# Sixteen layers on one core: batches normalised in the next layer's front, ternary layers as one stream, a cell with two gate bank sets

## The reference

```
x = x + f_i(layernorm(x))        # i = 0..15
layernorm(x) = (x - mean) / sqrt(var + 1e-5), over the 128 features
```

```
# layers 5, 7 (W1, W2 rounded to -1, 0, 1 beforehand)
h = relu(x @ W1.T + b1)          # 128 -> 512
out = h @ W2.T + b2              # 512 -> 128
# layers 13, 15: 32*64 tokens, here 4 batches of 512; the state c goes from batch to batch
f = sigmoid(x@wf.T + c@uf.T + bf); i = sigmoid(x@wi.T + c@ui.T + bi)
g = tanh(x@wc.T + c@uc.T + bc);    c = f*c + i*g
h = tanh(x@wo.T + c_final@uo.T + bo)   # once the last c is there, for all tokens
```

## Time and profile before

| | us |
|---|---|
| timed, 3 runs | 3011.98, 3024.86, 3028.07; median 3024.86 |
| profiled execution, its own time | 3016.8 |
| its span, first to last instruction | 3015.0 |
| TensorE busy | 2417.6 (80%) |
| VectorE busy | 1804.8 (60%) |
| ScalarE busy | 1277.7 (42%) |
| GpSimd busy | 644.2 (21%) |
| mean granted TensorE clock | 0.879 of full speed |

### The profile page before, as it was taken

How to read it: one execution, slowest core, us unless ns; L and a number is a source line. 1 busy time by engine, 2 the same in 40 slices (tenths; PEclk the granted TensorE clock), 3 DMA queues, 4 the chain that set the end, 5 groups by cost and what they waited for, 6 DMA issues and landing times. The chain is left out here.

```text
span 3015.0 us, 30344 instructions
## 1 busy us (share of the span) xinstructions
PE 2417.6 (80%) x9626; PEld 1001.7 (33%) x9626; DVE 1804.8 (60%) x2866; ACT 1277.7 (42%) x2512; POOL 644.2 (21%) x736
## 2 busy tenths in 40 slices
PE   8999999476699897776767399877779979777777
PEld 3333334122122343532333144322324437322223
DVE  5666654478777345424434644488884437378894
ACT  3555641276477312113222043265554312255562
POOL 1111110222111101100001010065551012055560
PEclk9999999688799998885669589888899979889889
DMA  3000000221000200000000000000000000000000
GB/s 137 1 1 1 1 1 1 32 38 17 1 1 1 84 1 1 1 0 0 0 0 1 0 0 0 1 0 1 1 0 1 0 1 2 1 0 0 0 1 14
DMA packets 9356, 25.90 MB, mean 9 GB/s; under 512 B 1072, under 2 KB 7280, under 8 KB 8176
## 3 DMA queue, kind: packets, MB, share of 16 engines
q1 hardware_dynamic: 8336, 23.18, 2.7%
q10 hardware_dynamic: 864, 0.79, 0.2%
HBM read 16.56 MB, written 1.05 MB: 6 GB/s over the span
## 5 line engine op out<-in xcount | busy, mean ns | idle before, releaser
L2599 PE MATMUL l_py<-l_read,w_const 128*128 128x512 f32 x512 | 316.3, 704 | 93.1 <-DVE l_read L2732 74.2
L2876 POOL TENSOR_TENSOR l_drive<-l_du,l_bsb 128x512 f32<-128x512 f32 x256 | 325.9, 1296 | 207.0 <-ACT l_bsb L2673 187.7
L2723 DVE TENSOR_TENSOR_SCAN l_state<-l_decay,l_drive 128x512 f32<-128x512 f32 x256 | 310.5, 1213 | 58.9 <-ACT l_decay L2681 51.4
L398 ACT ACTIVATE l_probs<-l_psp,l_stats 128x512 f32<-128x512 f32 x256 | 172.9, 682 | 150.6 <-DVE l_stats L408 150.6
L2681 ACT ACTIVATE l_decay<-l_delta,l_a 128x512 f32<-128x512 f32 x256 | 176.3, 689 | 136.1 <-DVE l_state L2723 135.7
L2599 PEld LDWEIGHTS l_py<-l_read,w_const 128*128 128x128 f32 x512 | 99.8, 215 | 246.9 <-DVE l_read L2732 204.1
L249 POOL TENSOR_TENSOR l_nx_small<-l_nx_small,w_const 128x4 f32<-128x4 f32 x27 | 27.2, 1009 | 717.2 <-DVE l_nx_small L243 717.2
L1267 DVE TENSOR_REDUCE l_tops<-l_ring 128x2 f32<-128x1024 f32 x128 | 151.5, 1220 | 46.0 <-PE l_ring L1258 45.6
L406 DVE TENSOR_REDUCE l_stats<-l_psp 128x2 f32<-128x1024 f32 x128 | 156.2, 1221 | 35.8 <-PE l_psp L360 35.1
L714 DVE SCALAR_TENSOR_TENSOR l_product<-l_psu,w_gated,l_first 128x512 f32<-128x512 f32 x104 | 78.1, 751 | 158.4 <-ACT l_first L688 158.1
L2732 DVE TENSOR_TENSOR l_read<-l_state,l_pc 128x512 f32<-128x512 f32 x256 | 168.4, 658 | 0.0
(11 more groups left out here) (510 smaller groups left out, 4624.7 us busy)
## 6 DMA issues: line engine op xcount, KB each, us to landing
l_stack<-l_parts SPq DMA_DIRECT2D x84, 64.0 KB
w_gated<-in_gated SPq DMA_DIRECT2D x1, 3297.5 KB, 10.5
w_mha<-in_mha SPq DMA_DIRECT2D x1, 2568.5 KB, 13.3
w_ssm<-in_ssm SPq DMA_DIRECT2D x2, 1171.0 KB, 15.6
w_moe<-in_moe SPq DMA_DIRECT2D x1, 2248.0 KB, 18.2
w_const<-in_const SPq DMA_DIRECT2D x1, 1325.0 KB, 7.6
x<-x_in SPq DMA_DIRECT2D x1, 1024.0 KB, 4.9
out<-x SPq DMA_DIRECT2D x1, 1024.0 KB, 3.9
```

Source lines behind the costliest of these rows:

```text
L398: act.activation(probs[:, s % 4, i, :], psp[:, s % 2, i, :], ACT.Exp, bias=stats[:, s % 4, 1, i:i + 1], scale=scale, accum_out=stats[:, s ...
L2599: pe.matmul(py[:, t, :], eye, read[:, s % 4, :], start=n == 0, stop=n == NS - 1, skip_group_check=True)\
L2723: dve.tensor_tensor_scan(state[:, s % 4, :], decay[:, s % 2, :], drive[:, s % 4, :], 0.0, ALU.mult, ALU.add).then_inc(L["state"].sem, 1)
L2876: pool.tensor_tensor(drive[:, s % 4, :], du[:, b % 2, t, :], bsb[:, n % 2, :], ALU.mult)\
```

## The change

- `NextNorm` can have more than one bank and then keeps a buffer per bank, so a batch's centre needn't wait for the norm of the one before.
- `NORMALISES_NEXT` gains 5 and 7, so the standalone norms n6 and n8 go; n0, n3, n7, n9, n11, n14 and n15 stay. `NORMALISES_LAST` gains 4, 5, 12 and 13: layers 3, 4, 11 and 12 normalise three batches, and layers 4, 5, 12 and 13 the fourth in their front (`late`, one centre to scale for batch 3).
- `routed_ffn`: scoring of the batches goes between the first up projections, and var, eps, spread and scale come one step later.
- `bit_ffn` is one stream of 16 steps over all batches with three buffers, two out banks and the norms inside, and reads xn without a copy.
- `cell` has two sets of gate banks, two answer banks and two h buffers; f*c is computed as soon as f is there.

The core of the diff ("..." for what is left out):

```diff
-    def __init__(self, L, bank, steps=1, last=False):
+    def __init__(self, L, *banks, steps=1, last=False):
...
+    def bank(self, b):
+        return self.banks[(b - self.first) % len(self.banks)]
+    def free(self, b):
+        return max(b - self.first - len(self.banks) + 1, 0)
...
# routed_ffn, TensorE
                 if last_in:
                     late.centre(pe, B - 1)
-                for b in range(B - 1):
-                    score(pe, b)
                 up(pe, 0)
+                up(pe, 1)
                 if last_in:
                     late.var(pe, B - 1)
-                up(pe, 1)
+                score(pe, 0)
                 up(pe, 2)
+                score(pe, 1)
                 if last_in:
                     late.spread(pe, B - 1)
                 up(pe, 3)
-                score(pe, B - 1)
+                score(pe, 2)
+                score(pe, 3)
...
-                    if normed(n, 3) is not None:
-                        nx.var(pe, normed(n, 3))
-                    if normed(n, 6) is not None:
-                        nx.spread(pe, normed(n, 6))
+                    if normed(n, 4) is not None:
+                        nx.var(pe, normed(n, 4))
+                    if normed(n, 7) is not None:
+                        nx.spread(pe, normed(n, 7))
... # VectorE: eps 4 -> 5, scale 8 -> 9; keep stays at 3, diag at 6
# linear_attention (4): centre first; var after project(0, 0); spread after turn_keys(0, 1);
#   VectorE keep ahead of the angles, eps after rotate(0, 0), diag after add_v(0), scale after take_states(0);
#   rstd on GpSimd after the MEMSETs. elu_attention (12) alike:
                     if is_batch(a):
                         project_q(pe, a)
                         project_k(pe, a)
+                        if a == 0 and last_in:
+                            late.var(pe, B - 1)
...
                     if is_batch(a):
                         turn_keys(pe, a)
+                        if a == 0 and last_in:
+                            late.spread(pe, B - 1)
...
                 pool.memset(state[:, :, :, :, :], 0.0).then_inc(L["blank"].sem, 1)
+                if last_in:
+                    late.rstd(pool, B - 1)
                 for a in range(B + 2):
...
# bit_ffn, new
+        def widen(pe, n):
+            b, m = divmod(n, FT)
+            if b == B - 1 and m == 0 and last_in:
+                pe.wait_ge(L["in_xn"].sem, L["in_xn"].at(0, 1))
+            pe.wait_ge(L["hidden"].sem, L["hidden"].at(0, max(n - 2, 0)))
+            pe.matmul(up[:, n % 3, :], w1[:, m * P:(m + 1) * P], core.xn[:, b * S:(b + 1) * S], start=True, stop=True)\
+                .then_inc(L["up"].sem, 1)
...
+                for n in range(END):              # END = N + 9
+                    if n < N:
+                        widen(pe, n)
+                    if 0 <= n - 2 < N:
+                        narrow(pe, n - 2)
+                    if n == 2 and last_in:
+                        late.var(pe, B - 1)
+                    if n == 5 and last_in:
+                        late.spread(pe, B - 1)
+                    if normed(n, 3) is not None:  # and centre 3, square 4, keep 4, var 5,
...                                               # eps and diag 6, spread 7, scale 8
# cell, new, TensorE
+                from_input(pe, 0)
+                from_state(pe, 0)
+                if last_in:
+                    late.var(pe, B - 1)
+                from_input(pe, 1)
+                if last_in:
+                    late.spread(pe, B - 1)
+                for b in range(1, B):
+                    from_state(pe, b)
+                    if b + 1 < B:
+                        from_input(pe, b + 1)
+                    else:
+                        answer_input(pe, 0)
+                        answer_input(pe, 1)
... # VectorE: late.diag and late.scale behind the first c
-NORMALISES_NEXT = (0, 1, 3, 4, 9, 11, 12)
-NORMALISES_LAST = (1, 3, 9, 11)
+NORMALISES_NEXT = (0, 1, 3, 4, 5, 7, 9, 11, 12)
+NORMALISES_LAST = (1, 3, 4, 5, 9, 11, 12, 13)
```

More of the change, by code:

```diff
@@ L1901, in _ @@
                         rotate(dve, a, 0)
+                        if a == 0 and last_in:
+                            late.eps(dve, B - 1)
                     if is_batch(o):
@@ L1906, in _ @@
                         add_v(dve, a)
+                        if a == 0 and last_in:
+                            late.diag(dve, B - 1)
                     if is_batch(o):
@@ L1984, in _ @@
             def _(pe):
[L1985 to L1993 removed]
+                if last_in:
+                    late.centre(pe, B - 1)
@@ L2002, in _ @@
                             .then_inc(L["hidden"].sem, 1)
+                    if normed(n, 4) is not None:
+                        nx.square(act, normed(n, 4))
             @block.vector
             def _(dve):
-                for b in range(B):
-                    take_normed(dve, L, b, xn[:, :])
-                    dve.wait_ge(L["down"].sem, L["down"].at(b, FT))
-                    dve.scalar_tensor_tensor(out=core.batch(b), in0=out[:, :], scalar=b2, in1=core.batch(b),
-                                             op0=ALU.add, op1=ALU.add).then_inc(L["done"].sem, 1)
+                if last_in:
+                    late.keep(dve, B - 1)
+                    late.eps(dve, B - 1)
+                    late.diag(dve, B - 1)
+                    late.scale(dve, B - 1)
@@ new lines, in _ @@
+                for n in range(END):
+                    if normed(n, 2) is not None or n == N + 2 and inner < B:
+                        b = (n - 2) // FT - 1
+                        x = core.x[:, b * S:(b + 1) * S]
+                        dve.wait_ge(L["down"].sem, L["down"].at(0, FT * (b + 1)))
+                        dve.scalar_tensor_tensor(out=x, in0=out[:, b % 2, :], scalar=b2, in1=x, op0=ALU.add,
+                                                 op1=ALU.add).then_inc(L["done"].sem, 1)
+                    if normed(n, 8) is not None:
+                        nx.scale(dve, normed(n, 8))
+                    if normed(n, 4) is not None:
+                        nx.keep(dve, normed(n, 4))
+                    if normed(n, 6) is not None:
+                        nx.eps(dve, normed(n, 6))
+                        nx.diag(dve, normed(n, 6))
@@ L2012, in bit_ffn, with _ @@
+            @block.gpsimd
+            def _(pool):
+                if last_in:
+                    late.rstd(pool, B - 1)
+                for b in range(inner):
+                    nx.rstd(pool, b)
     L.close()
@@ L2430, in _ @@
-                pe.wait_ge(L["state"].sem, L["state"].at(B - 1, 1))
-                for b in range(B):
-                    pe.wait_ge(L["answered"].sem, L["answered"].at(b, 0))
-                    pe.matmul(out[:, :], core.w(g, "wo"), core.normed(b), start=True, stop=False)
-                    pe.matmul(out[:, :], core.w(g, "uo"), c[:, :], start=False, stop=True)\
-                        .then_inc(L["answer"].sem, 1)
+                if last_in:
+                    late.centre(pe, B - 1)
@@ new lines, in _ @@
+                    dve.wait_ge(L["opened"].sem, L["opened"].at(0, 3 * b + 3))
+                    dve.tensor_tensor(ig[:, :], i_[:, :], n_[:, :], ALU.mult).then_inc(L["new"].sem, 1)
+                    dve.wait_ge(L["kept"].sem, L["kept"].at(0, b + 1))
+                    dve.wait_ge(L["new"].sem, L["new"].at(0, b + 1))
+                    dve.tensor_tensor(c[:, :], ig[:, :], h[:, 0, :], ALU.add).then_inc(L["state"].sem, 1)
+                    if b == 0 and last_in:
+                        late.diag(dve, B - 1)
+                        late.scale(dve, B - 1)
```

286 lines of the change are left out of this document (180 added, 106 removed).

## The result

The kernel after takes 2926.47 us (median of 4 runs, 2923.66 to 2933.32), the kernel before, run beside it, 3022.74; the ratio is 0.9689 with a 95% interval of 0.9657 to 0.9721. The forecast was 2929 us. In a later comparison the same code stood at 2918.53 against 3017.71, ratio 0.9675 (0.965 to 0.9699).

A forecast was written before the change was run, and what follows sets the result against it. Limits differ by place: TensorE in routed loops, engine-to-engine chains at tails and in the cell. Terms summed to -88.7 us from 3016.8, giving 2929 us; own range 2915 to 2943, wider range 2910 to 2960.

The forecast's parts named there:

- rival 1: Routed loops: the stall moves along with the later slots, so the loop saving is 0: 2958 us; chance 0.13.
- rival 3: Fronts wait as long as the old tails, so the norm stays on the path: about 2965 us; chance 0.05.
- rival 4: Slower: routed layers' steps run long at 1.2 GHz from cut scoring and denser TensorE work; 3049 us at 40%; chance 0.02.
- Rival 2: Routed and cell fronts keep a low clock: +3 instead of -8, layers 12, 13 2 us more each: 2944; chance 0.12.
- 1 and 2, tails and fronts: Tails of layers 3, 4, 11, 12 go: -39.3 us; moved norm costs +0.6 in layer 4, +2.2 in layer 12.
- the named cover: Layer 4's front: VectorE's late copy falls while the angles stand still for GpSimd's MEMSETs, so it costs 0.3 us.
- 3, ternary layers: Layers 5 and 7 as one stream, norm included: layer 5 51.0 us, 1.1 slower; layer 7 46.7 us, 1.8 faster.
- 4, routed loops: Layers 1, 3, 9, 11: later norm slots remove 24 TensorE stalls before variance and spread: -28.9 us, bounds 0 and 31.
- 5, routed fronts: Scoring between wide matmuls recovers half-clock loss in four fronts: -8 us of 10.2, layer 9 keeping 1.8; bounds -3 and 12.
- 6, the cell: Layers 13 and 15: rounds of 5.16, 5.16, 4.96 us instead of 6.19, answers 4.7 less: layer 15 -8.5, layer 13 -6.1.
- part 2: What the moved norm costs in the next layer's front: layer 4 +0.6 us, layer 12 +2.2 us.
- part 5: Routed layers' fronts by number, -8 us; the reference for layer 13's late norm cost, 2.4 us, means the cell.

The follow-up runs named there:

- e3: Kernel after, but layers 3, 4, 11 and 12 normalise their own last batch at their end again: 2951.29 us, ratio 0.9786.
- e5: Kernel after, with layers 6 and 8 also norming batches 0-2 inside, layers 7 and 9 taking the last, ternary copy before scale: 2902.99 us, ratio 0.9611.
- e1: Kernel after, with variance, eps, spread and scale of the routed loops put back one step earlier: 2962.3 us, ratio 0.9814.
- e7: Kernel after, with only spread and scale of the routed loops put back one step earlier: 2925.25 us.
- e8: Kernel after, with only variance and eps of the routed loops put back one step earlier: 2958.0 us.
- e2: Kernel after, with three batches of scoring again ahead of the first up projections in the four routed layers: 2934.3 us, ratio 0.9723.
- e4: Kernel before, with only the new cell and the one-stream ternary layers, nothing taken over: 2996.96 us against 3014.93, ratio 0.9929.

## Why the prediction was right

**The sum and what it stands on.** 2929 was forecast and 2926.47 measured, and rivals 1, 3 and 4 fell: the stalls did not move along (rival 1), the norm came off the path (rival 3, and e3), no loop ran at half clock (rival 4). Rival 2, a clock that stays low in the new fronts, fell in all four; in the fronts of layers 12 and 13, which it names too, half clock went from 30.7 to 20.5 us and from 14.8 to 3.4. That the profile's difference is so near the sum is partly luck: the changed stretches gave 101.1 us instead of 88.7, and 11.1 us came back in stages that the change does not touch (6.2 in layer 0, 7.0 in the norm ahead of layer 3, 2.7 and 2.2 around layers 10 and 14, less 6.7 in layer 1's tail and layer 2 and 0.3 in others). The timed ratio, 84 to 104 us by its interval, holds both sums.

**1 and 2, tails and fronts.** Layer 3 into 4, -8.9 as forecast, and by the named cover: the copy at 1134.82 falls under the MEMSETs. Layer 11 into 12 gave 8.0 instead of 6.8: the tail was 8.65 us where 9 was counted, the pow does stand ahead of kvar (2405.61 and 2406.68), but the spread and scale ahead of the first energies cost nothing, since these wait for kvar until 2413.45. That 1.2 us is no more than the clock moves this stretch.

**3, ternary layers.** 51.2 us for layer 5 from the last add of layer 4 (51.0 forecast), 46.4 for layer 7 (46.7). TensorE has no wait in the stream. The tail was forecast as 12.4 us from the last down matmul's end; it is 11.5 in layer 5 (1304.80 to 1316.34) and 11.9 in layer 7, with the chain that was named: the copy of batch 3 stands behind the scale of batch 2,

```profile
1308.95 0.69 DVE L279 TENSOR_TENSOR xn<-l_nx_kept,l_aux 128x512 f32<-128x512 f32 x1 [1.29 <-PE l_aux L271]
1309.55 0.68 DVE L235 COPY l_nx_kept<-l_first 128x512 f32<-128x512 f32 x1
1310.38 1.02 PE L242 MATMUL l_first<-w_const,l_nx_square 128*128 128x1 f32 x8 [1.54 <-DVE l_nx_kept L235]
```

and e5, which exchanges the two, has 2.2 us less.

**4, routed loops: the mis-sized term.** Forecast -28.9, measured -36.6. The mechanism was right (e1, e7, e8) and the stalls' own price too: 36.6 us less the 6.8 us that half clock took in the loops of the profile before is 29.8, against 28.9. What the forecast did not have is that part of the stalls cost a second time by the clock. It had taken the loop's clock as 0.99 and asked only whether denser work would lower it; the sign was the other way. The upper bound of 31 was passed for the same reason. In the trace of before the half-clock stretches inside the loops were there to be read, at 485.0, 1884.5, 2355.5 and 2399.9 us, 3.4 us each.

**5, routed fronts.** 11.1 instead of 8, inside the bounds. The step that was worked out low is the clock's return: layers 3, 9 and 11 have no half clock at all after their first matmul, where 1.8 us were kept for layer 9 and 2.2 taken off as a risk. In e1 and e8 layer 9 does pay 1.7, so the term is right and its size partly luck. The prediction read the earlier trace rows as a fall without a gap, and that reading is too strong: in the kernel before, too, layer 9's first scoring matmul (1753.68) had waited 1.49 us, 0.7 us inside the stretch that is shown, and the clock fell 1.1 us behind it. The Trainium skill, "TensorE: Matmul & The Clock Gate", section "Why this matters for your kernels", warns of idle gaps between bursts of matmuls. By that rule alone e2 would have given 0, since the gaps ahead of the fronts are alike (1.5 us in e2, 1.6 in the kernel after); it gave 13.2 us. In the loops long waits are alike too (up to 1.31 us ahead of a spread, 1.24 to 1.40 ahead of a variance), and only those ahead of the narrow variance brought the half clock: width and gap have to be read together.

**6, the cell** (which part 2 calls part 5 by a slip)**.** Layer 15 -8.9 (-8.5), layers 12's tail and 13 together -16.4 (-16.5). The rounds take 5.15 to 5.21 us (5.16, 5.16, 4.96 forecast), the answers 7.1 (7.1). In layer 13 the first round, with diag and spread of the late norm between, took 7.38 us from uf to uf, 2.2 over the others, where 2.4 were counted back. One reading of the old round is wrong, though its 6.19 us are right: 3.49, 1.33, 0.69 and 2.6 are not one chain, they add up to 8.1. In the trace of before wf starts as soon as the last gate is there, beside i*n, and not behind c:

```profile
2605.75 1.13 PE L2424 MATMUL l_ps_f<-xn,w_cell 128*128 128x512 f32 x2 [0.78 <-ACT l_n L2444]
```

So the old round is TensorE's own: 3.51 us from uf to that wf (three products and 0.78 us of waiting for the last gate) and 2.68 for wf, wi, wc. VectorE's 2.0 us up to c run beside them. The forecast for the new round didn't use the wrong step. The terms given for the new answers add up to 6.9, not 7.1; the 4.7 us saved were right.

## What to carry to other kernels

A norm (or any short chain over all engines) at a layer's end costs its whole chain, and in the middle of another batch's work only the time it takes on the engine that is the limit: 9 to 10 us against 0 to 2.6 here. Give each piece of such a chain a slot in the step after the one in which its input gets ready; TensorE's waits in a full loop are paid in full, and those ahead of narrow matmuls can be paid again by the clock (in e8 8.5 us on top of 14.8). When a layer has spare engine time (layer 6: nothing lost, 9.4 won behind it), put the norm inside it even if the layer itself is not the one being tuned.

## What the runs showed of the hardware

- Half clock from short waits ahead of narrow matmuls: at a layer's front, behind a wait of 1.4 to 1.5 us, 12 scoring products in a row (recorded as 24 matmuls) brought the granted clock to 0.66 to 0.90 while TensorE was 98 to 100% busy; with wide matmuls first, behind a wait of 1.6 us, three of the four fronts stayed at 1.00 in the kernel after. In the loops a variance of one column behind a wait of 1.24 to 1.40 us brought 3.4 us of half clock (1.7 us lost); a wait of 1.15 to 1.31 us ahead of a wide matmul did not in 24 cases.
- It does not happen each time: 18 of those 32 variances were hit. Layer 3's loop has the waits of layer 1's, and no such stretch in before, e1 and e4, but one in e8. Why one is hit and another not stays open.
- The same code of a stage takes different times in different profiles, by the clock: layer 0 takes 406.5 or 413.3 us, layer 3 up to its first add 78.6 to 85.6 (the seven profiles with the new front), the way to the first batch of layer 2 318.5 to 329.6. One profile against another tells a change of 10 us only stage by stage.
- At the start the granted clock reads 1.00 (nothing is recorded yet) while a pair of 128x512 matmuls takes 2.06 us; the duration, not the clock's row, tells the rate there.
